# A two-layer cross-attention kernel: a third place for turned probabilities, two buffers shared, and every engine's order written anew

## The reference

```python
# layer 0: 16 heads of 64
qn, kn, vn = ln(q), ln(k), ln(v)                      # q = x, k = v = ctx
attn = (qn @ Wq) . (kn @ Wk) + rel_bias[i - j]
p = softmax(attn / sqrt(64)); out = p @ (vn @ Wv)
x1 = q + out @ fc_w.T + fc_b
h = ln(x1)
x2 = x1 + gelu(h @ W1.T + b1) @ W2.T + b2
# layer 1: 16 query heads of 16, one key/value head, window of +-64 tokens
q, k, v = x2 @ Wq + bq, ctx @ Wk + bk, ctx @ Wv + bv
p = softmax(mask(q k^T / 4)); attn = (p @ v) @ Wo + bo
gate = silu([attn, x2] @ Wg + bg)
out = attn * gate + x2 * (1 - gate)
x_hat = out * rsqrt(mean(out^2) + eps) * rms_w
return x_hat - mean_over_tokens(x_hat)
```

## Time and profile before

| | us |
|---|---|
| median of 3 runs | 2022.23 (2021.83 to 2023.15) |
| the profiled execution | 2021.55 |
| its span, first to last instruction | 2019.8 |
| PE busy | 1892.9 (94%) |
| ACT busy | 1552.5 (77%) |
| DVE busy | 1510.7 (75%) |
| POOL busy | 1260.3 (62%) |
| mean granted TensorE clock | 0.981 of full |

### The profile page before, as it was taken

The page is one execution under the profiler, slowest core; times in us unless marked ns, Lnnn a source line. Parts: engine busy times, 40 slices in busy tenths (PEclk is TensorE's granted clock), DMA queues, the critical chain, the costliest instruction groups (busy, mean ns, idle before and its releaser), DMA issues.

```text
span 2019.8 us, 54925 instructions
## 1 busy us (share of the span) xinstructions
PE 1892.9 (94%) x18732; PEld 1717.0 (85%) x18732; DVE 1510.7 (75%) x6779; ACT 1552.5 (77%) x5588; POOL 1260.3 (62%) x1330
## 2 busy tenths in 40 slices
PE   8999999999999999999999999999999999999862
PEld 7888888889888888888888888888888988889752
DVE  4767778777777877777877777887777888777742
ACT  3588788777878787878887787878788887778842
POOL 2546666666666666666666666666566667666533
PEclk8999999999999999999999999999999999999976
DMA  6434444434444344344444444434434543443312
GB/s 197 126 79 106 117 117 99 115 102 102 107 123 110 94 108 113 95 117 117 102 113 101 103 105 124 110 97 118 107 92 114 124 110 98 110 112 85 83 47 50
DMA packets 215272, 214.49 MB, mean 106 GB/s; under 512 B 29904, under 2 KB 197456, under 8 KB 214992
## 3 DMA queue, kind: packets, MB, share of 16 engines
q1 hardware_dynamic: 214992, 210.97, 41.6%
HBM read 67.23 MB, written 9.44 MB: 38 GB/s over the span
## 4 chain that ended last, share of the span: by engine, by line
PE 40%; POOL 17%; DVE 15%; DMA 11%; SPq 8%; ACT 4%; issue 4%; ACTq 0%; POOLq 0%; DVEq 0%
PE bank L508 11%; PE bank L509 10%; PE bank L510 10%; SPq L203 8%; DMA soft<-turned 6%; DVE turned L193 6%; POOL soft L2714 5%; DMA raw<-in_x_t 4%; PE bank L644 3%; POOL cT L2768 2%; DVE hidS L1387 2%; PE bank L746 2%; POOL X L2777 2%; PE bank L631 2%; POOL raw L2723 1%
## 5 line engine op out<-in xcount | busy, mean ns | idle before, releaser
L193 DVE STREAM_TRANSPOSE turned<-soft 128x512 f32<-128x512 f32 x512 | 349.5, 696 | 139.6 <-POOL soft L2714 88.8
L2254 ACT ACTIVATE soft<-soft,row_min 128x128 f32<-128x128 f32 x1024 | 397.2, 392 | 48.4 <-DVE row_min L1419 48.4
L2178 ACT ACTIVATE soft<-soft,row_min 128x128 f32<-128x128 f32 x1024 | 399.1, 394 | 38.7 <-DVE row_min L1316 34.0
L2706 POOL TENSOR_TENSOR soft<-soft,inv_sum 128x512 f32<-128x512 f32 x256 | 272.5, 1065 | 219.3 <-DVE inv_sum L1324 187.3
L2714 POOL TENSOR_TENSOR soft<-soft,inv_sum 128x512 f32<-128x512 f32 x256 | 265.7, 1043 | 130.4 <-DVE inv_sum L1427 130.4
L1419 DVE CUSTOM_DVE_ANT_0 soft<-bank,winb 128x128 f32<-128x128 f32 x1024 | 226.1, 284 | 36.8 <-PE bank L733 36.7
L1316 DVE CUSTOM_DVE_ANT_0 soft<-bank,relb 128x128 f32<-128x128 f32 x1024 | 231.2, 281 | 9.7 <-PE bank L631 9.7
L2178 ACT ACTIVATION_READ_ACCUMULATOR soft<-soft,row_min 128x1 f32 x1024 | 195.7, 191 | 0.0
L2254 ACT ACTIVATION_READ_ACCUMULATOR soft<-soft,row_min 128x1 f32 x1024 | 194.4, 190 | 0.0
L508 PE MATMUL bank<-cT,wk 128*128 128x256 f32 x512 | 154.0, 301 | 31.5 <-POOL cT L2768 31.5
L508 PE MATMUL bank<-w,hidS 128*128 128x256 f32 x512 | 147.8, 289 | 12.7 <-ACT hid L2209 6.8
(11 more groups left out here) (191 smaller groups left out, 6744.4 us busy)
## 6 DMA issues: line engine op xcount, KB each, us to landing
soft<-turned SPq DMA_DIRECT2D x1024, 128.0 KB, 2.8
of_token<-stats_by_row SPq DMA_DIRECT2D x64, 256.0 KB, 3.8
tokens<-in_x SPq DMA_DIRECT2D x32, 256.0 KB, 3.6
tokens<-in_ctx SPq DMA_DIRECT2D x32, 256.0 KB, 3.4
raw<-in_x_t SPq DMA_DIRECT2D x32, 256.0 KB, 3.5
raw<-in_ctx_t SPq DMA_DIRECT2D x32, 256.0 KB, 2.7
X<-in_x SPq DMA_DIRECT2D x32, 256.0 KB, 3.1
out<-gate SPq DMA_DIRECT2D x64, 128.0 KB, 3.0
```

The source lines that it names most:

```text
L193: return eng.transpose(turned[:, slot, :, s % 2, :, :].rearrange("p j h b -> p h j b"), soft[:, s, :, :].rearrange("p h (j a) -> p h j a", ...
L2178: last = act.activation(soft[:, s, h, :], soft[:, s, h, :], ACT.Exp, bias=row_min[:, s, h:h + 1], scale=-1.0, accum_out=row_sum[:, s, h:h ...
L2254: last = act.activation(soft[:, s, h, :], soft[:, s, h, :], ACT.Exp, bias=row_min[:, s, h:h + 1], scale=-1.0, accum_out=row_sum[:, s, h:h ...
L2706: pool.tensor_tensor(soft[:, m % NS0, :, :], soft[:, m % NS0, :, :], inv_sum[:, m % NS0, :].unsqueeze(2).broadcast_to([P, QUAD, SEQ]), ALU ...
```

## The change

What it does, by buffers:

- `turned` gets a third slot. Layer 1's pair n uses slot 1 + n with a semaphore of its own, so `turn1` of a pair waits only for the spread of the same pair one batch earlier.
- `of_token` is no tile any more but a view of `tokens`: token rows and spread statistics of x and then of ctx go through the same 128 x 512 in turn. `tokens_x(g)` waits for `c_norm(g - 1)`, `tokens_c(g)` for `x_norm(g)`, `in_x` and `in_c` for the statistics taken from the tokens.
- `X` is gone: `load_x` writes into `x1`'s place of the group, `x_fcb` adds the bias there and `x1_sum` adds the bank to it. `load_x(g)` waits for `plus_x` of group g - 2 instead of `x1_sum` of g - 1.
- `bcol` lies in the third slot of `turned` in the setup.

And the orders: all five lists are new in the first part, the loop and the last part, and so is the choice of banks (bank 0 fixed, banks 1 to 7 rotating by one each turn). No product, no transfer and no operation is added or dropped. Inputs of group r + 2's x side, which were prepared in turn r, are now prepared as r + 1's in turn r; only `tokens_x(r + 2)` and `stats_x(r + 2)` stay at the end of the turn.

```diff
-        ring0 = banks[0:2]
-        ring2 = banks[2:8]
+        ring1 = banks[1:8]
-        X = sb("X", [P, GROUP, D])
         tokens = sb("tokens", [P, GROUP, D])
-        of_token = sb("of_token", [P, 2 * GROUP, SEQ])
+        of_token = tokens[:].rearrange("p b d -> p (b d)").rearrange("p (r n) -> p r n", n=SEQ)
-        turned = sb("turned", [P, 2, NB, 2, QUAD, BLOCK])
+        turned = sb("turned", [P, 3, NB, 2, QUAD, BLOCK])
...
             def load_x(g):
-                if g >= 1:
-                    till.wait_ge("x1", g)
-                sp.dma_start(X[:], ...)
+                if g >= 2:
+                    till.wait_ge("plus_x", GROUP * (g - 1))
+                sp.dma_start(x1[:, g % 2, :, :], ...)
             def tokens_x(g):
-                    till.wait_ge("stats_c", g)
+                    till.wait_ge("c_norm", g)
             def tokens_c(g):
-                till.wait_ge("stats_x", g + 1)
+                till.wait_ge("x_norm", g + 1)
...
-                spread(sp, 2 + n, 1, "spread1")
+                spread(sp, 2 + n, 1 + n, f"spread1_{n}")
...
-                if n >= 2:
-                    till.wait_ge("spread1", 16 * NB * (n // 2))
-                turn_blocks(dve, 1, NS0 + u).then_inc(sem["turn1"], 1)
+                if n >= NU1:
+                    till.wait_ge(f"spread1_{u // 2}", 16 * NB * (GROUP * g + b))
+                turn_blocks(dve, 1 + u // 2, NS0 + u).then_inc(sem["turn1"], 1)
```

More of the change, by code:

```diff
@@ L890, in tensor_program @@
-            mlp_out(1, 1, 0, banks[6])
-            mlp_out(1, 1, 1, banks[6])
-            out_mm(0, 1, banks[3], ("min0", 23))
-            turn_x2(1, banks[7], ("o1_lo", 2))
-            pv(2, 2, banks[1], ("min0", 24))
-            proj_q(3, 0, banks[6], ("x2", 2))
-            proj_q1(1, banks[4], ("y_out", 1))
-            proj_v(2, 3, banks[3], ("ag", 2))
-            scores1(1, 0, (banks[5], banks[4], banks[7], banks[6]), (("o_lo", 10),), (("q1_out", 2),), (("x2_lo",
-                2),), (("q_out", 13),))
@@ new lines, in tensor_program @@
+            proj_q(2, 0, banks[6], ("bias", 6))
+            turn_x2(0, banks[4], ("o_lo", 6))
+            fc(1, 1, banks[3])
+            proj_q1(0, banks[0], ("min0", 15))
+            pv(1, 2, banks[5], ("min0", 16))
+            scores1(0, 0, (banks[2], banks[0], banks[7], banks[4]), (("v_out", 7),), (("q1_out", 1),), (("x2", 1),),
+                (("x2_lo", 1),))
+            proj_v(1, 3, banks[6], ("q_out", 9))
+            kv_k(2, banks[5], ("o_lo", 7))
+            fc(1, 2, banks[3])
@@ new lines, in tensor_program @@
+            pv1(0, 0, 0, banks[4], ("min0", 19))
+            pv1(0, 0, 1, banks[4])
+            kv_v(2, banks[5])
+            scores1(0, 1, (banks[7], banks[0], banks[3], banks[6]), (("v_out", 9),), (("q_out", 11),), (("x1", 2),),
+                (("min0", 20),))
+            out_mm(0, 0, banks[2], ("k_out", 11))
+            pv(2, 0, banks[4], ("o1_lo", 1))
+            scores(2, 2, (banks[7], banks[0]), (("min1", 5),), (("min1", 6),))
+            proj_v(2, 1, banks[3], ("min1", 7))
+            turn_h(1, banks[2], ("ag", 1))
@@ new lines, in tensor_program @@
+            proj_k(NG - 3, 2, banks[7], ("min0", 235))
+            fc(NG - 4, 3, banks[5])
+            kv_v(NG - 3, banks[4])
+            pv1(NG - 5, 0, 0, banks[1], ("o_lo", 116))
+            pv1(NG - 5, 0, 1, banks[1])
+            center_out(NG - 6, 1, banks[0], ("v_out", 117))
+            scores1(NG - 5, 1, (banks[2], banks[6], banks[5], banks[7]), (("min0", 236),), (("q_out", 119),), (("x1",
+                29),), (("k_out", 119),))
+            out_mm(NG - 5, 0, banks[1], ("o1_lo", 55))
@@ new lines, in tensor_program @@
+            pv1(NG - 5, 1, 1, banks[5])
+            center_out(NG - 5, 0, banks[3], ("min0", 239))
+            mlp_out(NG - 4, 1, 0, banks[7])
+            mlp_out(NG - 4, 1, 1, banks[7])
+            out_mm(NG - 5, 1, banks[1], ("min0", 240))
+            turn_x2(NG - 4, banks[3], ("y_out", 55))
+            fc(NG - 3, 1, banks[6])
+            proj_q1(NG - 4, banks[2], ("o_lo", 118))
+            pv(NG - 3, 2, banks[5], ("o1_lo", 56))
+            scores1(NG - 4, 0, (banks[7], banks[1], banks[0], banks[3]), (("x2", 29),), (("ag", 56),), (("q_out",
+                121),), (("x2_lo", 29),))
@@ L1134, in tensor_program @@
[L1134 to L1141 removed]
+            turn_x2(NG - 1, banks[4], ("kv_turn", 32))
@@ L1924, in vector_program @@
[L1924 removed]
+            turn0(NG - 2, 5)
+            o1_lo(NG - 4, 1, banks[7])
             kv_out(NG - 3)
[L1926 to L1936 removed]
```

2290 lines of the change are left out of this document (1125 added, 1165 removed).

## The result

The changed kernel takes 1960.16 us (median, 1957.66 to 1962.68); the kernel before takes 2022.69. The ratio is 0.9688, with an interval of 0.967 to 0.9706: 3.1% faster, 62 us, where the prediction said 29. The profiled execution has a span of 1955.9 us, 63.9 less than before.

A forecast was written before the change was run, and what follows sets the result against it. TensorE was taken to bound the loop, leaving only its idle time to gain. Loop -24 (-29.5 - 11.4 + 9 + 4 + 4), head +3 and tail -8 gave -29 us, so 1993 us, range 1983 to 2012.

The forecast's parts named there:

- cT's wait: TensorE's loop wait for the context's low half before proj_k(r+1, 0): covered by fc and kv_k, -29.5 us.
- The spread's wait: Layer 1's turned probabilities: a place for each pair removes TensorE's wait, -11.4 us in the loop, 6.5 in the tail.
- the waits for the hidden layer (6.8) and for layer 0 (6.3): TensorE's loop waits for the hidden layer and layer 0's turned probabilities: taken as unchanged, bounds -13 and +26 us.
- (a): New wait at scores(r, 2) for min1 and y_out on VectorE: 0.35 late in 26 turns, +9 us.
- the sentence on the rule: VectorE's two variance steps: with GpSimd idle beside them both take 0.2 us, (a) is gone, sum 9 us lower.
- the third rival: More gain: none of (a), (b), (c) shows, with 198 ns for each variance step; 1976 us, chance 0.12.
- (b): New wait from proj_q1 to scores1(r-1, 0), covered only by pv(r, 2): 0.15 a turn, 29 turns, +4 us.
- (c): New waits from turn_x2 to proj_q1 and all such places: 0.15 a turn, +4 us.
- One buffer, in the loop: Tokens and spread statistics in one line: 29 us in a turn of 59, cover 1 us at pv(r, 2), cost 0.
- In the head, +3: One buffer delays the context's rows, so proj_k(0, 0) starts at 36.1 instead of 33.06: +3 us.
- The tail: -8 forecast: Three parts: last batch's spread 3.5 us sooner, batch before gains 3.0, proj_q1(31) no longer waits, 1.5: -8 us.
- The slower rival: Statistics' line late: loads lose 3.2 us, pv(r, 2) waits 2.1 a turn, +55 us, 2048 us; chance 0.20.

The follow-up runs named there:

- a_cov1: Changed kernel with proj_k(r+1, 0) moved ahead of fc(r, 2) in the loop, so only kv_k lies between proj_v(r, 3) and it: 1991.52 us, ratio 0.9848.
- a_cov0: Changed kernel with proj_k(r+1, 0) right behind proj_v(r, 3) in the loop, ahead of kv_k and fc(r, 2): 2055.83 us, ratio 1.0165.
- b_third: Kernel before with a third slot in turned for layer 1's second pair, orders unchanged, wq1 and wgx keeping only the high half: 1991.46 us, ratio 0.9838.
- a_bank: Changed kernel with one TensorE wait added: mlp_out(r-1, 0, 0) waits for hid_out(r-1, 2), as before the change: 1977.96 us, ratio 0.9771.
- b_swap: Kernel before with fc(r, 2) ahead of proj_k(r+1, 0), in the loop and the two groups after it: 2023.39 us, ratio 1.0.
- b_swap_v: Kernel before with b_swap's exchange, and on ScalarE v_out(r, 3) ahead of the two exps1 steps: 2022.32 us, ratio 0.9991.
- b_all: b_third plus both exchanges of b_swap_v (fc(r, 2) ahead of proj_k(r+1, 0), v_out(r, 3) ahead of the exponentials): 1988.83 us, ratio 0.9826.
- a_kout: Changed kernel with VectorE's k_out(r+1, 0) moved behind stats_x, turn1(r-1, 0, 0) and inv1(r-1, 0, 1) in the loop: 1992.25 us, ratio 0.9839.
- a_line: Changed kernel with the context's rows loaded twice in groups 4 to 29, SyncE waiting for the first load: 1990.79 us, ratio 0.9817.

## Why the prediction was off

**The direction and the loop's bound were right.** TensorE bounds the loop, and the gain is in its idle time. The two large waits went as said. cT's wait is near 0 (`proj_k` starts 0.14 behind the end of c_lo, 1052.45), the chain from the last read of cT is 2.1 us as counted, and `a_cov1` and `a_cov0` price the cover. The spread's wait went, and X's merge cost nothing that shows (no run takes it back alone).

**The step that failed is the sum.** It took every wait as a price of its own: two of the four go, two stay. In the kernel before that is not so in either direction. The cover alone gave 0 instead of 29.5. The place alone gave 31.7 instead of 18, since "the waits for the hidden layer (6.8) and for layer 0 (6.3) I leave as they are" missed that VectorE's stop in front of `turn1` delays `turn0` and `hid_lo`: with the stop alone gone (`b_third`) the two fell to 3.8 and 0.8. The rest of the hidden layer's wait went with the new order, where `a_bank` finds the choice of bank. The term's own bounds had these -13 us, but the range did not take them in. The profile's page had a hint: the chain had only 40% on TensorE. I read TensorE's busy share and its list of waits, and used the chain only for head and tail. The Trainium skill, Perfetto Trace Analysis, section Optimization Strategy, says to find the gaps of the most contended engine and make what they depend on come sooner. By that alone the time should have fallen in `b_swap` and `b_swap_v`, and it did not: two such gaps, 1.05 and 0.92 us in each turn, were closed, and the time stayed. The 13.1 us left standing are the first half of the miss in the loop.

**The new waits are the second half: +17 forecast, nothing on balance.** (Together 30 us; the miss in the loop is 26, since 50.3 came of the 54.0 with a name.) (a), +9: y_out is 0.86 early instead of 0.35 late. The difference, 1.2 us, is 0.62 for var_x and 0.56 for var2, which the prediction had in the sentence on the rule and the third rival in its sum; I took the rows, 0.78 and 0.73, for properties of the steps, when they were those of a neighbour. (b) and (c), +8: they exist. From the start of one product to the start of the next, the step from the end of the fc to `proj_q1` takes 0.36 us (0.12 before the change), the one from `pv(r, 2)` to `scores1` 0.38, and the one from `pv1(r - 2, 0, 1)` to `scores1` 0.41 (0.20 before). That is 0.6 us a turn where I had said 0.3, some 15 us in the 23 groups. (b) was right at 0.18; (c) was too small.

Why does so little of it show? The idle time without a name is 8.2 us in the 23 groups after and 1.6 before, but the busy time fell by 5.8 us for the same products. Part of that stood behind the old waits: there the next product starts after 0.22 us instead of 0.12, and this counts as busy. Counted from start to start, cT's step took 1.42 us instead of 0.20, so its wait held 28 us in the 23 groups and not 24.2, and the hidden layer's 7.9 and not 6.4. So what went was worth more than its idle time, and what came used that up; the match of 42.5 with 44.0 is partly luck.

**The rest of the loop is in the lists.** From `b_all` (1988.8) to the changed kernel (1960.2) lie 29 us that no single part gives. `a_kout` shows one of many places that carry them, worth 32 when undone alone. Which exchanges in the lists make up the 29 stays open: undone parts do not add up here any more than done ones.

**One buffer, in the loop: right.** No wait for the rows shows, and `a_line` finds the cover. **In the head, +3: wrong, 0.8.** `proj_k(0, 0)` starts at 33.90 instead of 33.06, not at 36. The x side ended at 16.9 and not 18.1 (its tokens are loaded first now), and c_lo then waited for ScalarE, which was at wv behind a load, as the chain of the head shows:

```profile
15.62 1.27 POOL raw L2721
...
22.19 1.97 DMA stats_by_row<-stat_rows
...
24.65 6.05 DMA soft<-in_wv_t
30.73 1.15 ACT wv L2119
31.88 0.52 ACT cT L2140
32.46 1.31 POOL cT L2760
33.90 0.36 PE bank L506
```

Of the 3.4 us up to product 1156 only 0.6 lie ahead of product 1000. Such differences carry no reading: kernels with the head of the kernel before reach product 1000 1.4 us (`b_third`) and 3.1 us (`b_all`) ahead of it.

**The tail: -8 forecast, -10.2.** The last batch is as worked out: its last reciprocal ends at 1931.58 and its spread has landed at 1938.04, 6.5 us later, where I had 6.3 and the kernel before 9.8. The third part was wrong: `proj_q1(31)` still waits 1.5 us for x2T. I had moved out_mm behind turn_x2 as a cover, but `x2_hi` waits for that out_mm, since it overwrites what out_mm reads, and the chain only starts behind it. So the first two parts and what else the new lists gave make up 10.2.

**The rivals.** The third, "none of (a), (b), (c) shows", came nearest with 1976. With the 13.1 us on top its sum is 1963. That this comes near 1960 is partly luck, since (b) and (c) did come. No rival had the waits that I left alone going away, and that is what the range lacked. The slower rival cost, by `a_line`, 1.2 us a turn once 3.2 us were added, but the line was not late.

## What to carry to other kernels

Before adding up the waits of the busiest engine, read what share of the chain that ended last it has, and take a low one as a warning. At 40% the closed gaps moved to the next name and the time stayed; at 72% (`b_third` to `b_all`) they did so, too. In the changed kernel, with 89%, the smaller delays that were put back (`a_cov1`, `a_kout`, `a_bank`) each cost about what their waits held. In that loop no gap was closed, so a high share is not shown to be a promise. When a buffer makes an engine stand in front of a landing, its price is not the wait it is named in but everything behind it in that engine's list, and it depends on the order (32 us in the old one; 258 in the new one, a part of it by the clock). Take a duration that differs from its twin's (0.78 against 0.20) as a sign of what ran beside it, and ask whether that neighbour is still there after the change.
